# Storing weighted adjacency pairs unturned, in 512-byte runs, with all blocks through DRAM

## What is computed

```python
# layer 1, attention over the edges into each node
alpha = (q_all[dst] * (k_all[src] + e)).sum(-1) * scale        # e = edge_attr @ We.T
w = exp(alpha - segment_max) / segment_sum
agg = segment_sum((v_all[src] + e) * w[:, None], dst)
# layer 2, weighted sum over neighbours
h = maximum(layernorm(x), 0)
AX = segment_sum(edge_weight[:, None] * h[src], node)          # node = first row of edge_index
x = x + AX @ W.T + b
```

## Time and profile before

| | us |
|---|---|
| three timed runs | 6184.1, 6188.63, 6187.37 |
| median | 6187.37 |
| span of the profiled execution | 5783.8 |
| median less span, what lies around it | 403.6 |
| PE busy / DVE / ACT / POOL | 5096.2 / 3797.7 / 2513.2 / 2089.2 |
| DMA moved, mean | 1046.25 MB, 181 GB/s |

### The profile page before, as it was taken

The page is one execution under the profiler, slowest core; times in us unless marked ns, Lnnn a source line. Parts: engine busy times, 40 slices in busy tenths (PEclk is TensorE's granted clock), DMA queues, the critical chain, the costliest instruction groups (busy, mean ns, idle before and its releaser), DMA issues.

```text
span 5783.8 us, 111605 instructions
## 1 busy us (share of the span) xinstructions
PE 5096.2 (88%) x41923; PEld 3729.9 (64%) x41923; DVE 3797.7 (66%) x6119; ACT 2513.2 (43%) x4924; POOL 2089.2 (36%) x2152
## 2 busy tenths in 40 slices
PE   1399999859999999999999999859999999879997
PEld 0276666528788877888788787625555555546665
DVE  4888888667767777777767776548888888420001
ACT  0266666446666666666666665622222222100001
POOL 5122201027777676776777666300000000001110
PEclk6699999979999999999999999979999999789998
DMA  7156665437777777777777777724344444156664
GB/s 212 67 200 204 209 203 190 150 131 193 206 200 202 204 202 198 205 201 200 203 199 206 201 197 199 239 83 182 148 178 163 175 172 162 46 167 203 208 205 120
DMA packets 821659, 1046.25 MB, mean 181 GB/s; under 512 B 468703, under 2 KB 693588, under 8 KB 793796
## 3 DMA queue, kind: packets, MB, share of 16 engines
q1 hardware_dynamic: 720232, 873.22, 45.9%
q0 software_dynamic: 87488, 151.98, 11.6%
q10 hardware_dynamic: 13407, 13.91, 0.9%
HBM read 637.29 MB, written 414.22 MB: 182 GB/s over the span
## 4 chain that ended last, share of the span: by engine, by line
PE 54%; SPq 17%; DVE 9%; DMA 9%; issue 5%; POOL 3%; ACT 3%; DVEq 0%; ACTq 0%; POOLq 0%
PE psum L1409 47%; DMA H<-local_dst_pairs 5%; DVE R L882 3%; SPq L653 3%; SPq L512 2%; PE psum L1631 2%; SPq L656 2%; DMA weighted_blocks<-R 2%; PE psum L1707 2%; SPq L650 2%; SPq L661 2%; SPq L490 2%; DVE H L882 1%; SPq L691 1%; POOL G L859 1%
## 5 line engine op out<-in xcount | busy, mean ns | idle before, releaser
L1409 PE MATMUL psum<-R,HT 128*128 128x384 bf16 x6076 | 1084.1, 326 | 59.8 <-DVEq L1398 59.8
L1409 PE MATMUL psum<-R 128*128 128x98 bf16 (+3 forms) x6858 | 974.6, 280 | 70.1 <-DVE R L882 27.8
L859 POOL DMA_INDIRECT G<-gather_table,cols_pc x908 | 868.0, 956 | 461.6 <-issue 255.0
L859 POOL DMA_INDIRECT H<-gather_table,cols_pc x896 | 856.1, 955 | 382.9 <-issue 256.7
L1774 ACT ACTIVATE H<-psum 128x512 f32<-128x512 f32 (+1 forms) x752 | 419.7, 558 | 1217.0 <-PE psum L1409 671.1
L1774 ACT ACTIVATE HT<-psum 128x784 bf16<-128x784 f32 (+2 forms) x1079 | 711.0, 677 | 381.4 <-PE psum L1409 308.1
L1774 ACT ACTIVATE R<-psum 128x512 f32<-128x512 f32 (+2 forms) x1257 | 710.5, 587 | 354.7 <-PE psum L1707 160.3
L1409 PEld LDWEIGHTS psum<-R,HT 128*128 128x128 bf16 x6076 | 566.7, 97 | 383.4 <-DVEq L1398 60.1
L1409 PE MATMUL psum<-R,l 128*128 128x512 f32 (+1 forms) x1647 | 728.9, 524 | 8.6 <-DMA R<-attr_parts 5.9
L882 DVE TENSOR_TENSOR HT<-HT,psum 128x512 f32<-128x512 f32 (+1 forms) x949 | 602.1, 653 | 181.2 <-PE psum L1409 175.8
L1409 PEld LDWEIGHTS psum<-R 128*128 128x128 bf16 (+1 forms) x6858 | 562.7, 111 | 225.1 <-issue 36.8
(11 more groups left out here) (244 smaller groups left out, 7327.8 us busy)
## 6 DMA issues: line engine op xcount, KB each, us to landing
weighted_blocks<-R SPq DMA_DIRECT2D x252, 512.0 KB
adjacency_blocks<-HT SPq DMA_DIRECT2D x74, 1568.0 KB, 5.6
ACC<-weighted_blocks SPq DMA_DIRECT2D x28, 3136.0 KB, 10.4
R<-weighted_blocks SPq DMA_DIRECT2D x28, 3136.0 KB, 10.4
HT<-adjacency_blocks SPq DMA_DIRECT2D x50, 1568.0 KB, 6.6
H<-local_dst_pairs SPq DMA_DIRECT2D x113, 512.0 KB
R<-attr_parts SPq DMA_DIRECT2D x451, 99.0 KB
weighted_blocks<-ACC SPq DMA_DIRECT2D x84, 512.0 KB
```

The lines of the kernel that those rows point to most:

```text
L859: pool.indirect_dma_start(out=slot(p)[:, 0:F], out_offset=None, in_=table, in_offset=edge).then_inc(s_g[p // GR % 8], 16)
L1409: return nc.tensor.matmul(o, lhs_t, rhs, start=start, stop=stop)
```

## The change

Operands of a build are swapped: `hw` (98 wide) is the stationary operand and `hs` is streamed (128 columns), so that a pair comes out as [98, 128 nodes], the layout that `send` reads. No block is turned. `copy_weighted` copies [98, 512] into one of three staging buffers per chunk, and `store_pairs` writes a chunk of 16 pairs to DRAM, four per block, 98 x 16 runs of 512 bytes. All 74 blocks go through DRAM: the late ones (now the last 18) are built in the third layer during the sends of the first 54 blocks, stored and loaded. Loads see the same 25 KB per partition as before. X stays in place, with no copy in DRAM.

```diff
-    bw_d = dram("weighted_blocks", [NPRE, P, W * P], f32)
+    bw_d = dram("weighted_blocks", [NBK, 64, J, P], f32)
...
+        staged = [HT[0:J, k * HB * P:(k + 1) * HB * P] for k in range(3)]
+        staged2 = [hflat[0:J, k * HB * P:(k + 1) * HB * P] for k in range(3)]
...
+        STEPS = GN + 5
+        LATE = NPL * 16
+        SENDS = NB * (NPRE - 2)
+        def builds_until(n):
+            return PRE_N + min(LATE, (LATE * n + SENDS - 1) // SENDS)
         def builds_after(n):
+            return range(builds_until(n), builds_until(n + 1))
+        def one_hots_at(q):
+            return 4 * (q - PRE_CH) * SENDS // LATE - 9
...  # sync
-            sp.dma_start(keep_d, X[:, :, :]).then_inc(s_x, 16)
...
-            def store_turned(i, h):
-                first, end = 8 * P * h, min(NP, 8 * P * (h + 1))
-                c = HALVES * i + h
-                sp.wait_ge(s_te, NB * i + min(NB, 2 * h + 2))
-                sp.dma_start(bw_d[i][:, first:end], staged[c % 4][:, 0:end - first]).then_inc(s_bst[c % 4], 16)
+            def store_pairs(c):
+                sp.wait_ge(s_we, 4 * c + 4)
+                o = (staged if c < PRE_CH else staged2)[c % 3]
+                sp.dma_start(bw_d[c // 4][HB * (c % 4):HB * (c % 4 + 1)].rearrange("q m c -> m q c"),
+                             o.rearrange("m (q c) -> m q c", c=P)).then_inc(s_bst[c % 3], 16)
...
-                for i, turned in turns_in(k - 6):
-                    if turned % 2 == 1 or turned == NB - 1:
-                        store_turned(i, turned // 2)
+                if k % 2 == 1 and (k - 11) // 2 in range(PRE_CH):
+                    store_pairs((k - 11) // 2)
...
-            sp.dma_start(X[:, :, :], keep_d).then_inc(s_x, 16)
...
             def load_block(i):
                 if i >= 2:
-                    sp.wait_ge(s_tm, NB * (block_of(i - 2) + 1))
-                sp.dma_start(BW_load[i % 2], bw_d[i]).then_inc(s_al[i % 2], 16)
+                    sp.wait_ge(s_tm, NB * (i - 1))
+                if i >= NPRE:
+                    for k in range(3):
+                        sp.wait_ge(s_bst[k], 16 * len(range(k, 4 * i + 4, 3)))
+                sp.dma_start(BW_load[i % 2], bw_d[i].rearrange("q (d w) c -> (q d) (w c)", d=2)).then_inc(s_al[i % 2], 16)
...
-            for i in range(2, NPRE):
+            for i in range(2, NBK):
                 load_block(i)
+                while stored < ALL_CH and 4 * stored + 4 <= builds_until(NB * (i - 1)):
+                    store_pairs(stored)
+                    stored += 1
...  # tensor, build_weighted
-                        last_ins = mm(psum[:, bank, k * P:k * P + J], hs[:, q % 2, r // 2, :, r % 2],
-                                      hw[q % 2][part][:, r // 2, :, r % 2], start=part == 0, stop=part == 2)
+                        last_ins = mm(bank4(bank)[0:J, k, :], hw[q % 2][part][:, r // 2, :, r % 2],
+                                      hs[:, q % 2, r // 2, :, r % 2], start=part == 0, stop=part == 2)
...
-            def turn_beside(i, g):
...
-            t.wait_ge(s_x, 96)
+            t.wait_ge(s_x, 64)
...
-            def turn(n):
...  # scalar, copy_weighted
+                c, i = n // 4, n % 4
+                if i == 0 and c >= 3:
+                    act.wait_ge(s_bst[c % 3], 16 * (c // 3))
+                o = (staged if n < PRE_N else staged2)[c % 3]
+                activation(o[:, i * 4 * P:(i + 1) * 4 * P], psum[0:J, (1, 2, 7)[n % 3] if n < PRE_N else n % 3, :], ACT.Copy).then_inc(s_we, 1)
...
-            def copy_turned_beside(i, g):
...
-            def copy_turned(n):
```

More of the change, by code:

```diff
@@ L79, in gnn_kernel @@
     PRE_N = PRE_CH * 4
[L80 to L82 removed]
+    ALL_CH = NBK * 4
+    ALL_N = ALL_CH * 4
     AK = W + 2
@@ L331, in gnn_kernel @@
         at += P * HB
-        staged += [r1[:, at + k * 8 * P:at + (k + 1) * 8 * P] for k in range(3)]
-        assert at + 3 * 8 * P <= NR1 and 4 * J * HB == NP == W * F
+        assert at <= NR1 and NP == W * F
         H3T = r1[:, 0:NP]
@@ L462, in gnn_kernel @@
         s_pc = [sem("pair_columns_loaded0"), sem("pair_columns_loaded1")]
-        s_bst = [sem(f"turned_windows_stored{k}") for k in range(4)]
-        s_tt = sem("sources_turned")
-        s_te = sem("turned_sources_copied")
+        s_bst = [sem(f"weighted_pairs_stored{k}") for k in range(3)]
         s_tm = sem("sources_multiplied")
@@ L718, in _ @@
             sp.wait_ge(s_wb, PRE_N)
-            for k in range(4):
-                sp.wait_ge(s_bst[k], 16 * len(range(k, HALVES * NPRE, 4)))
-            sp.wait_ge(s_tt, PRE_T)
+            for k in range(3):
+                sp.wait_ge(s_bst[k], 16 * len(range(k, PRE_CH, 3)))
             for c in range(4):
@@ L742, in _ @@
             sp.dma_start(by_partition(table)[:, 0:W, :], H).then_inc(s_tab, 16)
-            for i in range(2, NPRE):
+            stored, wanted = PRE_CH, NPRE + 2
+            for i in range(2, NBK):
                 load_block(i)
-                if i % 3 == 1 and 2 <= i // 3 + 1 < NPL:
-                    load_columns(NPRE + i // 3 + 1)
+                while stored < ALL_CH and 4 * stored + 4 <= builds_until(NB * (i - 1)):
+                    store_pairs(stored)
+                    stored += 1
+                while wanted < NBK and one_hots_at(4 * wanted) <= NB * (i + 2):
+                    load_columns(wanted)
+                    wanted += 1
+            assert stored == ALL_CH and wanted == NBK
             sp.wait_ge(s_h, 4)
@@ L1595, in _ @@
             t.wait_ge(s_att, 1)
-            def wait_for_bank(c):
-                if c >= 3:
-                    kind, before = made[c - 3]
-                    t.wait_ge(s_we if kind == "build" else s_te, before + 1)
             def build_weighted(n):
@@ L1957, in _ @@
                     activation(GT[:, k % 2], bank4(0), ACT.Copy).then_inc(s_gt, 1)
-                for i, g in turns[0:1]:
-                    copy_turned_beside(i, g)
-            for i, g in turns_in(STEPS - 1)[1:2]:
-                copy_turned_beside(i, g)
-            for k in range(4):
-                act.wait_ge(s_bst[k], 16 * len(range(k, HALVES * NPRE, 4)))
+            for k in range(3):
+                act.wait_ge(s_bst[k], 16 * len(range(k, PRE_CH, 3)))
             copy_blocks(2, AGT)
@@ L1971, in _ @@
             act.wait_ge(s_tab, 48)
[L1973 to L1985 removed]
+            for m in range(PRE_N, ALL_N):
+                copy_weighted(m)
             layer_norm(3)
```

132 lines of the change are left out of this document (17 added, 115 removed).

## The result

| | before | after |
|---|---|---|
| timed runs, us | 6184.1 to 6190.29 (4) | 6064.94, 6066.87, 6077.98, 6080.36 |
| median | 6188.0 | 6072.42 |
| ratio, 95% interval | | 0.9819 [0.9805, 0.9833] |
| span of the profiled execution | 5783.8 | 6063.3 |

The account below looks back on a forecast made before the run. Prediction: transfers holding back SyncE's queue bound attention, TensorE the layer behind. Sum: 6187.4 + 246 (stores) - 93 (layer behind) - 8 (seam) = 6332 us, 2.3% slower; range 6090 to 6490, likeliest case 6230 to 6450.

Parts of the forecast that it names:

- The first step: Whole kernel: 403.6 us of the 6187.4 median lie around the profiled span of 5783.8 and stay unchanged.
- the term for attention: Attention: the new stores' cost on SyncE's queue, 4.4 us per block over 56 blocks, +246 us.
- Item 3: Attention stores: four of 512-byte runs per block delay SyncE's queue and the load VectorE awaits; +246 us, bounds +62 to +370.
- Item 4: Attention staging buffers: ScalarE's copy waits for the store of three chunks before; taken as covered, no cost counted.
- rival 3: Attention: the staging wait takes over, ScalarE stands 448 us in place of the 246; 6534 us, chance 0.12.
- Item 1: Attention: 49 transposes per block removed relieve TensorE of 7.8 us per block; none counted, at most 218 us in all.
- Item 2: Builds: each matmul streams 128 columns, not 98; 0.07 us per build taken, 0.15 if streaming sets the pace.
- Item 5: Seam between attention and the layer behind: sums' load no longer held back, X load gone; about -4 each, -8 us.
- Item 6: Layer behind attention: turns go, builds move in; 14.6 us per block for 54, 10.7 for 20; -93, bounds -125 to -55.
- rival 1: Attention: stores absorbed, 6148 us, or 6086 if the 14 engines cost nothing either; chance 0.18.

Follow-up runs that it names:

- e1: The kernel before, unchanged, profiled once more: 6190.2 us, span 6188.7.
- e3: The kernel after with stores of weighted pairs left out after the first four chunks, every block load reading the first block: 6036.1 us.
- e5: The kernel after with every second gather left out from the 33rd edge row on, two per step in place of four: 5964.9 us.
- e13: The kernel before with every second gather left out, two per step in place of four: 5738.7 us.
- e2: The kernel before with one transpose in place of four in each turn beside attention; copies, stores and waits stay: 6157.4 us.
- e9: The kernel after with GpSimd waiting for the products once per eight gathers instead of once per four: 6799.1 us.
- e10: The kernel before with GpSimd waiting for the products once per eight gathers instead of once per four: 7197.4 us.
- e11: The edit of e9 and e10 with one wait for the products per sixteen gathers: 7261.4 us.
- e7: The kernel after with one matmul of each build's twelve left beside attention from the 17th build on: 6235.1 us.
- e12: The kernel after with three of the four gathers of a step, the fourth left out from the 33rd edge row on: 6022.3 us.
- e14: The kernel before with three of the four gathers of a step: 5787.7 us.
- e18: The kernel after with every second gather left out and only the first four chunks stored, all block loads reading the first block: 5253.4 us.

## Why the prediction was wrong, step by step

- **The first step failed: "403.6 us lie around the span. I take them as unchanged."** They were 6.5% of the time, and no row showed what they held. In e1 and in after 1.6 us lie around the span. 383 of them were the difference between the attention step of the profiled execution (5.40 us) and of the timed ones (6.25). By this the term for attention, +246 in the sum, was read from a limit that the timed runs don't have: measured, attention changed by -30. Everything read about attention, the waits, the chain and the queue, described an execution without the hold.
- **Item 3, stores, +246:** without effect in the timed regime (at most 36 of after's time, by e3). Without the hold its size is within its bounds (+315 for the whole change in attention, by e5 and e13), but only half of its way is right: SyncE's queue is held up behind the stores (20.2% of e5's chain), yet not through load_rows, whose wait grows by 63 us; that the sum came within the bounds is in part luck. The issue of the sums behind a store takes 2.8 to 3.4 us in SyncE's queue, as item 3 priced with 2.4. SyncE's queue in after:

```profile
2104.62 0.47 SPq L660 DMA_DIRECT2D weighted_blocks<-HT  x1
2105.30 2.84 SPq L632 DMA_DIRECT2D attention_sums<-H  x1
...
2117.94 0.47 SPq L660 DMA_DIRECT2D weighted_blocks<-HT  x1
2118.61 3.39 SPq L632 DMA_DIRECT2D attention_sums<-H  x1
```

  It is there in the timed regime too, and nobody waits for it, since the sums' store has eight steps of room and VectorE's load comes early within a step of 6.2 us.
- **Item 4, staging three deep, "I take it as covered":** wrong without the hold. ScalarE waits 782 us for stores in e5, 124 in e13 (98.5 + 25.8). That is over the 400 us that the prediction named as the sign of rival 3; its mechanism is in that regime a good part of the 315, at less than its price of 448. With the hold the wait is absent.
- **Item 1, turns, counted zero:** right for the timed kernels, within 33 us (e2), but for another reason than the half of the group spent on SyncE and VectorE.
- **Item 2, swapped operands:** a build costs 0.69 us in the third layer (from 4301.85 to the next send at 4302.54), against 0.61; taken 0.07 more, measured 0.08. The 12.5 ns for 30 columns, and with them the bound of 0.15 us per build, agree with the trace of before: from 480 to 600 us, at a granted clock of 1.00, bf16 matmuls of 384 columns start 162 ns apart and those of 98 columns 46 ns (medians), 12.2 ns for 30 columns or 2.5 columns a nanosecond, where the item has 2.4.
- **Item 5, seam, -8:** the last product to the load of the sums takes 4.2 us in place of 9.2, and the first product follows that load after 26.4 us in place of 30.3: -8.9, as forecast. A second 9.4 us came that I hadn't seen, and it lies in TensorE's clock behind the wait for X that is now gone (22 us at 0.57 are 9.5 lost). First before (e1), then after, each with its first product in the timeline and the stretch that begins with it:

```profile
4163.08 2.04 PE L1409 MATMUL psum<-H,WT 128*128 128x512 f32 x2 [3.96 <-issue]
```

```profile
4163.00:4185.00 22.00, 21.92 (x26) 6.49 (x26) 0.00 (x0) 2.97 (x8) 0.00 (x0) 0.57 0.27 114
```

```profile
4123.76 1.12 PE L1385 MATMUL psum<-H,WT 128*128 128x512 f32 x2 [0.36 <-ACT R L1703]
```

```profile
4124.00:4140.00 16.00, 16.00 (x33) 5.19 (x33) 0.00 (x0) 3.89 (x10) 0.00 (x0) 1.00 0.51 202
```

  In e1 the products behind an idle stretch of 3.96 us run at a mean granted clock of 0.57, and the first two take 2.04 us; in after, where TensorE stood only 0.36 us, they run at 1.00 and take 1.12. That the idle time lowers the clock is my reading of these two stretches; no run changed it alone.
- **Item 6, third layer, -93:** measured -77. With builds a block takes 44.4 / 3 = 14.8 us (taken 14.6), and the remaining 20 blocks (1020.3 - 54 x 14.8) / 20 = 11.1 (taken 10.7). Both excesses are small: 11 and 7 us. The load of a block lands in 11.0 us against 10.4.
- **The rivals:** the time, 6072, is next to rival 1's second value (6086: stores absorbed, engines free). Its mechanism, 27% of free engine time, is not what happened: in the regime of the profile the stores weren't absorbed at all. The point of decision was not in the list: that the step hangs on something that neither loads nor stores touch.

## What to carry to other kernels

Set the profile's span against the timed runs before reading any row: where a fifteenth of the time is missing from the profile, its stages may be those of another execution, and the missing time must have a place before a sum is built on it. A cost that is real (here 3.2 us a store) is worth nothing where another delay covers it, and a large one as soon as that is mended: the layout of before, with 4 KB runs, is the better one in attention once the hold is gone, by 327 us with three gathers a step (2736.4 against 2409.6; 235 of the whole kernel, since the third layer gains in either case). An engine at work must not be relieved on trust: less work for TensorE cost 163 us here (131 net of the chip).

## What the runs showed of the hardware that was not expected

- TensorE's completions can come late, or its work be held up, while GpSimd issues indirect gathers. In runs with four in a row the product's semaphore is 2.0 us (e1) to 3.9 us (e3) late in the median; with eight in a row every second one by 7 us (e9, e10), with sixteen every fourth by 15 (e11); e7, with fours and eights mixed, has a quarter late; with three or two the median is 0.01 to 0.07 us (e12, e14, e5, e13, e18). TensorE's idle time without a wait goes with it: from 1400 to 3500 us, 256 us in e1 and 341 in after on the line of the products, 48 in e5, 6 in e13.
- The gathers' closeness doesn't decide it alone. They are issued 1.25 us apart in all of these, and the first profile of before had runs of 12 to 32 of them with no late completion on record. The cause is open; a run that issues the same rows by fewer instructions would tell the number of instructions from the bytes.
- The kernel before ran without the hold in the one execution that the first profile recorded (span 5783.8) and took 6182.8 to 6220.1 us in every timed run: the same program has two speeds in attention, 5.40 and 6.25 us a step. What decides between them stays open too.
- With eleven of a build's twelve matmuls left out (e7) the granted clock of the stage went from 0.95 to 0.82 and the time up by 163 us. That the clock is the cause is argued, not shown: no run changed the clock alone, and GpSimd's gathers there often came in runs of eight, where after has four.
- None of the runs with the full computation beat the kernel after beyond noise.
